# A long-convolution block on one core: where the feed-forward steps, folds and evictions stand beside the convolutions

## The reference

```
x + (xn + conv_mixer(xn)) + ffn(xn)
conv_mixer: proj = (layernorm(xn)*gamma + beta) @ W_in + b_in, cut into v, x1, x2 (256 features each)
            y = causal_conv(v, k0) * x1 ;  y = causal_conv(y, k1) * x2      (128 taps per feature, along the tokens)
            y @ W_out + b_out
ffn:        (silu(xn @ wg.T) * (xn @ wu.T)) @ wd.T      (hidden width 768, integer weights times 1/127)
```

## Time and profile before

| | |
|---|---|
| median of 3 runs | 375.74 us (375.56 to 376.61) |
| the profiled execution, its own time | 376.25 us |
| its span, first to last instruction | 374.4 us |
| PE, DVE, ACT, POOL busy | 314.0, 253.6, 183.2, 196.6 us |
| mean granted TensorE clock | 0.945 of full |

### The profile page before, as it was taken

The page is one execution under the profiler, slowest core; times in us unless marked ns, Lnnn a source line. Parts: engine busy times, 40 slices in busy tenths (PEclk is TensorE's granted clock), DMA queues, the critical chain, the costliest instruction groups (busy, mean ns, idle before and its releaser), DMA issues.

```text
span 374.4 us, 11762 instructions
## 1 busy us (share of the span) xinstructions
PE 314.0 (84%) x4940; PEld 244.9 (65%) x4940; DVE 253.6 (68%) x522; ACT 183.2 (49%) x383; POOL 196.6 (53%) x268
## 2 busy tenths in 40 slices
PE   0637593988699889999999999999997997857995
PEld 0426462877477667677777777777765775645994
DVE  1894994788356766666667657667658666576986
ACT  1465363896253434433534444434443344427993
POOL 3697085466566746747657667567564573210000
PEclk9977867899899999999999999999999899996999
DMA  8996100033268758687786786886886768500345
GB/s 251 340 306 218 65 1 4 2 92 137 56 242 374 249 218 320 256 321 279 268 355 237 283 355 227 306 333 222 315 315 247 268 202 339 199 0 3 115 168 170
DMA packets 22072, 81.00 MB, mean 216 GB/s; under 512 B 2050, under 2 KB 13186, under 8 KB 13826
## 3 DMA queue, kind: packets, MB, share of 16 engines
q1 hardware_dynamic: 21026, 79.04, 57.7%
q10 hardware_dynamic: 992, 1.18, 1.0%
HBM read 75.50 MB, written 4.72 MB: 214 GB/s over the span
## 4 chain that ended last, share of the span: by engine, by line
DVE 28%; ACT 18%; POOL 17%; PE 17%; issue 15%; DMA 3%; POOLq 0%; DVEq 0%; SPq 0%; ACTq 0%
PE bank_c L270 6%; DVE sgh L830 6%; ACT hhl L613 5%; DVE vx L721 4%; POOL vx L999 3%; PE bank_g L270 3%; PE bank_u L270 3%; ACT vx L663 3%; POOL x1y L1068 3%; DMA res<-in_L_attn_x 3%; DVE ybuf L851 3%; POOL ybuf L1062 3%; DVE hhl L835 2%; DVE res L842 2%; POOL vhl L1005 2%
## 5 line engine op out<-in xcount | busy, mean ns | idle before, releaser
L270 PE MATMUL bank_d<-wd,hhl 128*128 128x256 f16 x384 | 87.3, 271 | 4.5 <-DVE hhl L835 4.1
L270 PEld LDWEIGHTS bank_p<-wq,xT 128*128 128x128 f16 x1536 | 72.4, 99 | 18.2 <-issue 2.2
L270 PE MATMUL bank_p<-wq,xT 128*128 128x64 f16 x1536 | 82.2, 195 | 1.8 <-issue 1.8
L270 PEld LDWEIGHTS bank_c<-vhl,bands 128*128 128x128 f16 x1024 | 52.7, 98 | 28.5 <-issue 13.4
L270 PE MATMUL bank_c<-vhl,bands 128*128 128x64 f16 (+3 forms) x1024 | 61.4, 187 | 10.2 <-POOL vhl L1005 7.9
L270 PE MATMUL bank_u<-xT,wgu 128*128 128x512 f16 x192 | 66.7, 381 | 0.0
L270 PE MATMUL bank_g<-xT,wgu 128*128 128x512 f16 x192 | 66.7, 381 | 0.0
L270 PEld LDWEIGHTS bank_c<-ybuf,bands 128*128 128x128 f16 x1024 | 51.7, 96 | 19.2 <-issue 3.2
L270 PE MATMUL bank_c<-ybuf,bands 128*128 128x64 f16 (+3 forms) x1024 | 60.1, 184 | 2.7 <-DVE ybuf L855 2.7
L835 DVE TENSOR_TENSOR hhl<-sgh,hhl 128x512 f16<-128x512 f32 x48 | 39.0, 812 | 34.1 <-ACT hhl L613 34.1
L613 ACT CAST hhl<-sgh 128x512 f16<-128x512 f32 x48 | 29.6, 617 | 54.9 <-DVE sgh L830 54.6
(11 more groups left out here) (167 smaller groups left out, 541.6 us busy)
## 6 DMA issues: line engine op xcount, KB each, us to landing
bands<-taps_seq SPq DMA_DIRECT2D x64, 1024.0 KB, 7.6
out<-res SPq DMA_DIRECT2D x8, 512.0 KB, 2.9
res<-in_L_attn_x SPq DMA_DIRECT2D x3, 1024.0 KB, 10.4
res<-in_L_attn_x SPq DMA_DIRECT2D x2, 512.0 KB, 8.3
bands<-in_L_attn_W_in ACTq DMA_DIRECT2D x1, 768.0 KB, 5.7
bands<-in_L_ffn_w_gate SPq DMA_DIRECT2D x1, 768.0 KB, 10.0
bands<-in_L_ffn_w_up SPq DMA_DIRECT2D x1, 768.0 KB, 10.2
vx<-in_L_ffn_w_down SPq DMA_DIRECT2D x1, 768.0 KB, 10.5
```

What stands on the lines that cost most here:

```text
L270: return nc.tensor.matmul(o, w, m, start=start, stop=stop, skip_group_check=True)
```

## The change

`LATE = 2` moves the feed-forward steps two places later: group G has steps 3G-2, 3G-1, 3G, those below 0 are left out, and steps 46 and 47 stand behind the last convolution, step 45 beside it. In the last two groups `convolve_ahead` puts two channels ahead of each of the 8 gate and up parts, and the down parts behind all channels. The down parts of step 47 stand behind the transposes of the first two y blocks, inside the branch. The wait for all feed-forward weights moves from ahead of the loop to group 0's projection. On VectorE the second eviction of the first convolution moves ahead of `split_h` (in the last two groups ahead of `hidden`), the second `scale_bank` ahead of `split_h`, and `fold` from even groups to odd groups, behind that eviction. On ScalarE the second `copy_lo` moves ahead of `round_h`. On GpSimd both `add_bias` stand ahead of both `split_v`. The preparation of the output weights is cut into five functions, in groups 8, 10, 12, 14 and 15, and the reduction of the maxima over the first 15 groups is done in group 15. The diff shows TensorE, ScalarE, VectorE and GpSimd in this order; the line numbers of the changed kernel differ from those of the kernel before.

```diff
+    LATE = 2
...
+            def convolve_ahead(G, v, n, general):
+                for i in range(8):
+                    conv_channel(G, v, 2 * i)
+                    conv_channel(G, v, 2 * i + 1)
+                    ffn_part(n, i, general)
+                for i in range(8, 16):
                     ffn_part(n, i, general)
...
             def body(general):
                 for b in range(FORK, NB + 4):
                     first_stage(b)
-                pe.wait_ge(unit_h, PAIRS)
-                pe.wait_ge(unit_l, PAIRS)
                 for G in range(NG):
+                    n = SG * G - LATE
                     if G == NG - 2:
                         find_wo_max()
-                    if G == 0:
-                        ffn_step(0, general)
-                        convolve(0, 0)
+                    if G < NG - 2:
+                        convolve_beside(G, 0, n, general)
                     else:
-                        convolve_beside(G, 0, SG * G, general)
+                        convolve_ahead(G, 0, n, general)
                     if G == NG - 2:
                         spread_wo_max()
-                    project_beside(banks_of(G), SG * G + 1, general)
+                    project_beside(banks_of(G), n + 1, general)
+                    if G == 0:
+                        pe.wait_ge(unit_h, PAIRS)
+                        pe.wait_ge(unit_l, PAIRS)
                     if G < NG - 1:
-                        convolve_beside(G, 1, SG * G + 2, general)
+                        convolve_beside(G, 1, n + 2, general)
                     else:
-                        convolve(G, 1)
-                        ffn_step(SG * G + 2, general)
-                for n in (STEPS - 2, STEPS - 1):
-                    for i in range(8):
-                        down_part(n, i, general)
-            FORK = 17
-            for b in range(FORK):
-                first_stage(b)
-            pe.wait_ge(ffn_consts, 1)
-            general = pe.value_load(flag[0:1, 0:1], min_val=0, max_val=1)
-            with pe.If(general > 0):
-                body(True)
-            with pe.Else():
-                body(False)
+                        convolve_ahead(G, 1, n + 2, general)
+                for n in range(STEPS - LATE, STEPS):
+                    ffn_step(n, general)
+                for i in range(8):
+                    down_part(STEPS - 2, i, general)
+                pe.wait_ge(wo_ready, 1)
+                pe.wait_ge(y2_ready, 2 * NG)
+                transpose_y(0)
+                transpose_y(1)
+                for i in range(8):
+                    down_part(STEPS - 1, i, general)
...
-                elif b == 2:
-                    pe.wait_ge(folded, 2 * NCHUNK)
+                elif b >= 2:
+                    pe.wait_ge(folded, 2 * NCHUNK - 3 + b)
...
+                n = SG * G - LATE
+                if G < NG - 2:
+                    ffn(n, [silu])
+                    copy_lo(G, 0, 0)
+                else:
+                    copy_lo(G, 0, 0)
+                    ffn(n, [silu])
                 copy_lo(G, 0, 1)
-                round_y1(G)
-                silu(SG * G + 1)
-                round_h(SG * G + 1)
+                if G < NG - 2:
+                    ffn(n, [round_h])
+                    round_y1(G)
+                else:
+                    round_y1(G)
+                    ffn(n, [round_h])
+                ffn(n + 1, [silu, round_h])
                 if banks_of(G) is not None:
                     round_v(banks_of(G))
                 if G < NG - 1:
-                    silu(SG * G + 2)
-                copy_lo(G, 1, 0)
+                    silu(n + 2)
+                    copy_lo(G, 1, 0)
+                else:
+                    copy_lo(G, 1, 0)
+                    silu(n + 2)
                 if banks_of(G) is not None:
                     round_v(banks_of(G) + 1)
                 if G < NG - 1:
-                    round_h(SG * G + 2)
-                copy_lo(G, 1, 1)
+                    round_h(n + 2)
+                    copy_lo(G, 1, 1)
+                else:
+                    copy_lo(G, 1, 1)
+                    round_h(n + 2)
+            silu(STEPS - 2)
+            round_h(STEPS - 2)
             silu(STEPS - 1)
-            round_h(STEPS - 1)
...
+            scale_y(0)
+            round_h(STEPS - 1)
+            scale_y(1)
...
             for G in range(NG):
+                n = SG * G - LATE
                 if G == NG - 2:
                     diagonal_of_maxima()
-                if G > 0:
+                if G == NG - 1:
+                    link(token_max(G - 1))
+                elif G > 0:
                     token_max(G - 1)
                 add_halves(G, 0, 0)
-                hidden(SG * G)
-                split_h(SG * G)
-                add_halves(G, 0, 1)
-                split_y1(G)
+                if G < NG - 2:
+                    if n >= 0:
+                        hidden(n)
+                    add_halves(G, 0, 1)
+                else:
+                    add_halves(G, 0, 1)
+                    hidden(n)
+                if G >= 3 and G % 2 == 1:
+                    fold((G - 3) // 2)
+                if G < NG - 2:
+                    if n >= 0:
+                        split_h(n)
+                    split_y1(G)
+                else:
+                    split_y1(G)
+                    split_h(n)
                 if banks_of(G) is not None:
                     scale_bank(banks_of(G))
-                hidden(SG * G + 1)
-                split_h(SG * G + 1)
-                if G >= 2 and G % 2 == 0:
-                    fold(G // 2 - 1)
+                if n + 1 >= 0:
+                    hidden(n + 1)
                 if banks_of(G) is not None:
                     scale_bank(banks_of(G) + 1)
+                if n + 1 >= 0:
+                    split_h(n + 1)
+                if G == NG - 8:
+                    output_scales()
+                if G == NG - 6:
+                    output_weights()
                 if G == NG - 4:
-                    output_weights()
+                    output_maxima()
+                if G == NG - 2:
+                    scale_output_weights()
                 if G == NG - 1:
                     split_output_weights()
+                    nc.vector.tensor_reduce(earlier, ymax[:, 0:NG - 1, :].rearrange("p g b -> p b g"), AX.X, ALU.max)
                 add_halves(G, 1, 0)
                 if G < NG - 1:
-                    hidden(SG * G + 2)
-                    split_h(SG * G + 2)
-                add_halves(G, 1, 1)
-            token_max(NG - 1)
-            hidden(STEPS - 1)
-            split_h(STEPS - 1)
-            dve.wait_ge(ymax_ready, NG)
+                    hidden(n + 2)
+                    split_h(n + 2)
+                    add_halves(G, 1, 1)
+                else:
+                    add_halves(G, 1, 1)
+                    hidden(n + 2)
+            link(token_max(NG - 1))
+            split_h(STEPS - 3)
+            hidden(STEPS - 2)
             dve.wait_ge(bout_added, NB)
-            link(nc.vector.tensor_reduce(st[:, 2, :], ymax[:, :, :].rearrange("p g b -> p b g"), AX.X, ALU.max))
+            link(nc.vector.tensor_tensor(st[:, 2, :], earlier, ymax[:, NG - 1, :], ALU.max))
             link(power_of_two(st[:, 0, :], st[:, 2, :], TOP))
             nc.vector.tensor_scalar(st[:, 1, :], st[:, 0, :], c(C_OS), None, ALU.mult).then_inc(st_ready, 1)
+            split_h(STEPS - 2)
+            hidden(STEPS - 1)
             dve.wait_ge(st_ready, 1)
             link(nc.vector.reciprocal(st[:, 1, :], st[:, 1, :]))
+            split_h(STEPS - 1)
...
                     add_bias(banks_of(G))
+                    add_bias(banks_of(G) + 1)
                     split_v(banks_of(G))
-                    add_bias(banks_of(G) + 1)
```

56 lines of the change are left out of this document (28 added, 28 removed).

## The result

The changed kernel takes 361.77 us (median of 4 runs, 361.16 to 362.69), the kernel before 375.65 (375.05 to 376.61) beside it. The ratio is 0.964 (0.960 to 0.969). The profiled execution takes 361.94 us, its span is 360.2 and its mean granted clock 0.957. The forecast was 361.4 us and a span of 360.05.

A forecast was written before the change was run, and what follows sets the result against it. The prediction took TensorE to bound the middle, with waits on other engines' chains making groups differ. Seven terms summed to 14.35 us, taking the median from 375.74 to 361.4 us; own range 359.9 to 363.4, chance 0.52.

The forecast's parts named there:

- Term 1: The start: group 1 begins at 108.1 instead of 110.25, gaining 2.15 us; bounds 1.0 and 2.6 if nothing waits.
- term 2: Group 1: one down part fewer and a shorter wait at its end gain 1.15 us; bounds 0.9 and 1.5.
- term 3: Groups 2 to 11: waits before even groups go, one issue wait of 1.8 stays, gaining 4.6 us; bounds 0 and 6.4.
- Term 4: Groups 12 and 13: spreading the output weights removes a wait and the lower clock following it, gaining 4.1 us.
- term 5: Group 14: paired convolutions and an earlier eviction, less 0.35 for scaling output weights, gain 1.25 us; bounds 0.4 and 2.3.
- term 6: Group 15 to the last stage's first rounding: earlier scale, partly lost to late steps, gains 0.4 us; bounds -1.6 and 1.7.
- term 7: Last stage: full clock on TensorE, with only short gaps before it, gains 0.7 us; bounds 0 and 0.8.
- Rival F: Group 2's issue wait of 1.8 us goes too, being a matter of code position: 359.6 us; chance 0.05.
- Rival B: Waits before even groups stay, from late round_v or from fold and split_y1 delaying the scaling: 366.0 us; chance 0.20.
- rival E: Slower: in odd groups VectorE stops at the fold, holding up split_y1 and scaling; 377 us and more; chance 0.03.
- rival D: In the tail the two late steps are not hidden and the last stage's clock gain stays away: 364.1 us; chance 0.08.
- Rival C: In the last stage, TensorE's jump out of the branched body costs 0 to 2.8 us: about 363.7; chance 0.10.

The follow-up runs named there:

- run 9: The changed kernel with the loads of bands for groups 1 to 3 cut to one channel of eight each (output differs): 360.24 us, ratio 0.961.
- run 1: The kernel before with only the bank order changed: second scale_bank ahead of split_h, both add_bias ahead of both split_v: 373.99 us, ratio 0.998.
- run 2: The kernel before with the second scale_bank ahead of split_h in odd groups only, GpSimd's order as before: 374.03 us, ratio 0.998.
- run 3: The kernel before with only the early eviction: VectorE's second eviction ahead of split_h, ScalarE's copy_lo ahead of round_h: 371.78 us, ratio 0.990.
- run 6: The kernel before with only the preparation of the output weights spread over groups 8, 10, 12, 14 and 15: 373.63 us, ratio 0.996.
- run 7: The kernel before with the bank order changed on VectorE and GpSimd and the output weights' preparation spread: 372.40 us, ratio 0.992.
- run 8: The kernel before with the early eviction and the spread output weights, without late steps, moved fold or channel pairs: 368.00 us, ratio 0.982.
- run 4: The changed kernel with the bank order undone on VectorE (second scale_bank behind split_h) and GpSimd (as before): 361.86 us, ratio 0.964.
- run 5: The changed kernel with only GpSimd's order undone (add_bias, split_v, add_bias, split_v): 362.57 us, ratio 0.966.
- run 10: The changed kernel with step 0's gate and up ahead of group 0's first convolution instead of beside its second: 362.09 us, ratio 0.965.
- run 12: The changed kernel with the last stage's first two transposes behind step 47's down parts and the jump out of the branched body: 365.19 us, ratio 0.973.
- run 11: The changed kernel with step 0 in the starting wait, group 14's residuals behind the gates and scale_output_weights ahead of split_y1: 363.20 us, ratio 0.967.

## Why the prediction was right, and where it was not

By its own terms, forecast and measured in the profiled execution (us gained):

```
term                        forecast  measured   from
1 start                       2.15      2.21     110.25 - 108.04
2 group 1                     1.15     -0.79     14.75 - 15.54
3 groups 2 to 11              4.6       5.51     147.30 - 141.79
4 groups 12 and 13            4.1       4.12     32.27 - 28.15
5 group 14                    1.25      1.44     13.85 - 12.41
6 group 15, first rounding    0.4       0.89     21.73 - 20.84
7 last stage                  0.7       0.82     34.25 - 33.43
sum                          14.35     14.20
```

**Terms 2 and 3.** The step that failed is in term 2, "its wait at the end shrinks": it left out the issue wait, which term 3 kept in group 2. It moved into group 1 (1.65 and 0.21 us) and term 2 turned negative; term 3 gained 1.8 of it back, less 0.56 in group 3 (its issue wait) and 0.47 in group 8 (a late eviction). It is not the whole miss: in run 9, without any issue wait, group 1 still takes 14.08 us, a gain of 0.67 and not 1.15, with a wait of 0.19 us for y1 in it and one of 0.37 for v at its end. Rival F, the wait as "a matter of where code stands", is refuted by run 9: it comes with the band traffic. The kernels 1 to 3 and 6 to 8 have TensorE's code of before, instruction for instruction, and show 0, 0, 0, 0.85, 0 and 0 us of it where before shows 1.84. (The profile also writes "issue" at the start of four even groups in run 3 and one in run 8, 0.15 to 0.17 us each; they come 0.26 us after the last split of v ends, the same hand-over as from 184.91 to 185.17 before, so they are counted as waits for v.)

**Term 3's mechanism.** Size right, cause half wrong. I gave the gain to the scaling "ahead of split_h instead of behind it" and to add_bias, which "no longer waits behind a split". Runs 4 and 5 show both to be worth nothing in the changed kernel. Run 3 shows that the early eviction alone brings y1, hidden, split_h and the second scaling forward by 0.57 us and takes that much off the wait of 0.9; in run 4, with the late steps and the moved fold as well, they come 1.37 earlier and the wait is gone. What was right is the next limit: ScalarE's round_v behind copy_lo, last split_v forecast at g + 13.8, measured 13.73 in the changed kernel and in run 4. In group 7 the eviction came at g + 4.82 (forecast 4.75), the fold ended at 6.57 (6.5), split_y1 at 7.76 (7.9). Rival B named this same limit and did not come to pass; rival E (a fold that holds up split_y1) neither: no wait for split_y1 stands in an odd group. But run 1 shows how near a late fold is in even groups: 1.14 us each. Moving it needs the steps to be late, since only then does a chunk's last down part land just ahead of an odd group's eviction.

**Term 4.** The sum is right to 0.02, its two parts are not as told. I put 1.6 of it to a lower clock "that followed" the idle time. Between starts of first convolutions the two groups take 32.38 us before, 31.69 and 31.26 in runs 2 and 3 with the same idle time at full clock, and 29.06 in run 6 without it. So the clock is 0.7 to 1.1 of the term, and some 3 are the wait and what stood around it. The dip is shown in one execution of the kernel before; its other executions have mean clocks from 0.936 to 0.954 around this one's 0.945, and whether they dip in the same group no row shows. "Each in VectorE's idle time" was right only for the changed kernel: with folds in even groups the same operations cost 2.4 us in groups 8 to 11 (run 6).

**Term 1.** Right, but with no slack behind it. Run 10 shows TensorE and the eviction chain ending within 0.35 us of each other, so "2.6 if nothing waits" could not have been reached by TensorE alone.

**Terms 5 to 7.** The ninth channel waited 0.48 (forecast 0.7), the fold ran from 5.47 to 6.87 (5.7 to 7.0), the second convolution began at 7.89 (7.95), the last evictions at 11.99 (12.4), the first scaling by the new scale began at 17.8 (18.1), scale_y(1) began at 19.56 (20.1) and the first rounding at 20.84 (21.35). The half microsecond begins with VectorE's instructions ahead of the last evictions, which I had counted 0.4 too long. Against run 8, which has neither the late steps nor the moved fold nor the pairs of channels, the stretch from group 15 on is 0.64 us longer. That would fit two steps behind the last convolution that are nearly but not wholly hidden, rival D by this much, but no run has the late steps alone. The forecast compared with a kernel whose output weights stood there.

**Rival C**, the jump: refuted twice, in the changed kernel and in run 12, where it stands ahead of the first transpose. The Trainium skill, "Runtime: NRT & Kernel Launch", section on instruction fetch mechanics, says that a taken branch to code outside the fetched pages stalls until that code is loaded. Neither row has a stall, which agrees if the target was already there; no row shows whether it was. The prediction's price for this rival does not follow from its own bounds: with 0 to 2.8 us the middle is 362.8, not 363.7.

**The sum** is closer than its terms, and that is luck: term 2 fell 1.94 us short, and terms 3, 5 and 6 brought 0.91, 0.19 and 0.49 more. Most of the first two is one issue wait that changed places, 1.84 us in group 2 before and 1.86 in group 1 after. (In term 3, 140.8 + 1.8 is 142.6, not 142.7.)

Not tried: the late steps alone with everything else as before. The fold's place depends on them, so they can't be separated without a third order of folds.

## What to carry to other kernels

Look for the instruction that stands early in a long chain over several engines and try that one first: here an eviction of 0.4 us moved ahead of a split gave two thirds of what the bank order had been credited with. Spreading small operations helped here only where a stretch had lost something else: the same six operations cost 1.1 us in a group that kept its fold (run 6) and 0.5 in one that had lost it. A change in several parts is judged part by part in both directions, added to the old kernel and taken out of the new one, since in one context two orders work only together and in the other neither matters. And compare stretches before medians: an issue wait or a dip of the clock of 1 to 2 us in a stretch that no edit touches is as large as most effects here.

## What the runs showed of the hardware

TensorE can wait for its own instructions behind data. In the changed kernel three waits (0.21, 1.65 and 0.40 us) end 2.1 to 2.7 us after a 16 KB packet of instructions begins (at 106.8, 114.8 and 141.2 us), with 403 GB/s moving in the window from 113 to 118 us; not every packet is followed by a wait (the one at 120.2 is not); with loads of an eighth of the size the packets begin up to 5.0 us earlier and no wait is left. The Trainium skill, same page and section, says that instruction fetch is hidden because instructions are dispatched more slowly than the fetch fills; these rows differ, and the measurement decides.

The clock: 2.32 us of idle time went with a mean granted clock of 0.89 in the next group in one kernel and with 1.00 in two others that had 2.28 and 2.32. In group 1, waits of 1.50 and 0.50 us went with a mean clock of 0.60 from 109.8 to 114.0 in run 11, and waits of 1.50 and 0.52 with 1.00 from 109.0 to 114.0 in run 10.

VectorE and GpSimd slow each other on some operations in SBUF: split_h takes 0.69 us alone and 1.18 beside GpSimd's gate (175.63 in the kernel before), GpSimd's bias addition 1.07 alone and 1.45 beside split_h (205.11 in the changed kernel), and two scalings of the output weights that took 0.62 took 1.05 beside the residuals in run 11. The Trainium skill, "SBUF — State Buffer", section "Who interferes with whom", says that a VectorE instruction with two SBUF inputs contends with a GpSimd instruction that reads SBUF, and the rows agree for split_h.
